# Attention's tail takes up the first slots of sequence 0 and turns six sequences' tokens, in a fused transformer block on one core

## The chip, the cores and the metric

The kernel runs on one core of a Trainium2 chip. The metric is the device time of one execution, in microseconds; the median of three runs before the change is 558.34 us (557.69 to 560.09).

## The reference, cut to what matters

Eight sequences of 256 tokens with 192 features, all in fp32, pass through three residual parts. First a token mixer with one attention head (the embedding is gathered, two layer norms over the whole sequence). Then an attention with 12 heads of 16 features, whose queries and keys are RMS-normed. Last a two-level soft mixture of experts. The change stands between the last two parts, so these are what must be seen:

```
h = h + attn(layernorm(h))          # 12 heads: softmax(q k) v, then a projection
xg = l2norm(layernorm(h)) * sqrt(192) * gamma_in   # groups of 64 tokens
phi = l2norm(slots1) * sqrt(192)                   # 128 slots
logits1 = xg @ phi.T
disp1 = softmax(logits1, over the 64 tokens)       # dispatch
comb1 = softmax(logits1, over the 128 slots)       # combine
slots = disp1.T @ xg;  yn = l2norm(slots) * sqrt(192) * gamma2
... second-level slots, 32 experts, and comb1 mixes their output back
```

## The kernel before, in words

The program is a sequence of blocks: `mixer_and_attention`, `first_slots`, `second_slots`, `second_dispatch`, `experts`. In a block each engine has its own instruction list, written out by hand, and waits on semaphores; an engine executes its list in order. A block ends when all engines have ended their lists, and the next begins together on all of them.

**Attention.** One sequence n is one call of `body(n)` on PE, ACT and DVE, and the bodies overlap by hand. Twelve heads are three quads of four heads, a quad q is two pairs u of two heads. `scores_and_maxima(score, best)` (L579 to L618) issues for one pair the plain products whose row maxima DVE wants (L604, into PSUM banks `MAXES` = 0, 1) and for an earlier pair the products with the maximum folded in (L611, into `SCORES` = 2, 3). DVE's `row_max` (L1141) reduces a pair's 128x1024 products. When a quad's two pairs have their maxima, PE's `turn_max` (L626) transposes them through bank 2 and DVE's `keep_max` (L1146) writes them into the queries. ACT's `expo` (L916; L920 in two halves for the second pair) takes the exponentials out of banks 2 and 3 into `prob`. PE's `mix` (L643) multiplies them by the values into banks 4 and 5. The next quad's `expo` waits for the `mix` of the quad before, since `prob` has one buffer for each pair; the next pair's scores wait for the `expo` of the pair before, since there is one pair of score banks. After a sequence's third `mix` come `keep_out` (ACT, L925), `turn_out` (PE, L653), `divide` (DVE, L1153 and L1157), `turn_mixed` (PE, L662), `keep_mixed` (ACT, L930), `project` (PE, L672), `add` (DVE, L1164), `out_stats` (DVE, L1172 and L1175), `root_out` (ACT, L936 and L939) and `make_tokens` (POOL, L330 and L334). In `body(n)` these steps of sequence n-1 are interleaved with the quads of n, as are the steps that make the queries, keys and values of n+1, which use banks 6 and 7 (`FRONT`).

In the last body, n = 7, there is no next sequence, and `keep_busy` (L97, matmuls of the identity whose results nobody reads) stands in those places; it stands too between all steps behind it (L758 to L769). After `project(7)` PE issues ten of them, and the block ends with `root_out(7)` on ACT. POOL has made tokens 0 to 6 by then.

**First slots.** For each n, PE turns the tokens (`turn`, L1350, into bank 3, `TURN`), ACT copies them (`keep`, L1459), PE makes the logits (`logits`, L1365, banks 1, 2 or 6, 7), DVE takes their maxima (`maxima`, L1528 and L1530), ACT the exponentials for dispatch (L1468) and combine (L1476), PE turns the dispatch weights (`turn_disp`, L1384, bank 3), DVE copies them (L1546) and inverts the sums (L1535), POOL scales the combine weights (`scale_comb`, L1611), PE turns these (`turn_comb`, L1375, bank 3) and DVE copies them (L1539). PE makes the slots (`make_slots`, L1395), ACT squares them (L1486) and takes their factors (L1491, L1494), DVE norms them (`norm_slots`, L1552). PE averages and turns them. The list is a loop over n (L1427) in which iteration n holds `logits(n)`, `turn(n + 2)`, `make_slots(n - 1)`, `turn_comb(n - 1)`, `make_means(n - 2)` and `turn_disp(n)`. POOL makes the tokens of sequence 7 (`make_x`, L1600 and L1604) before the first `scale_comb`. SP issues three loads of 576 KB for the second slots when the block begins.

## Time and profile before

| what | value |
|---|---|
| median of 3 runs | 558.34 us (557.69 to 560.09) |
| the profiled execution | 555.03 us |
| its span in the trace | 553.3 us |
| mean granted TensorE clock | 0.997 |
| attention's last body to the end of its block | about 239.9 to 271.5 us |
| first slots | 271.5 to 326.0 us |
| second slots, second dispatch | 326.0 to 409.5 us |
| experts and the end | 409.5 to 553.3 us |

Times in the views are microseconds from the start of the span. PE is TensorE's matmul, PEld its weight load, DVE VectorE, ACT ScalarE, POOL GpSimd, SP SyncE. "PEclk" is the clock that TensorE was granted, 1.00 being full. A matmul of fp32 operands shows as two instructions, so the counts of PE are twice those in the code. Matmuls are pipelined: the duration of a group of them reaches a little into the next group, so where the order is plain the starts of two groups are the better measure. In brackets stands the engine's idle time ahead of an instruction and what ended it.

### The profile page before, as it was taken

To read this page: it belongs to the slowest core of one execution; us is meant where nothing else is said; L and a number is where in the kernel's file an instruction comes from. 1 tells how busy PE (TensorE), PEld (TensorE's weight loads), DVE (VectorE), ACT (ScalarE), POOL (GpSimd) and SP (SyncE) were. 2 spreads that over 40 slices of the span, in tenths; PEclk is the share of its full clock that TensorE was granted. 3 is DMA by queue.
4 is the path that set the end of the run, shared out by engine and by line. 5 is a ranking of instruction groups with operands and counts; after the bars stand their busy time and mean duration, and the time that the engine had idled before them with its cause. 6 is when DMAs were issued, how large, how long until landed. Compare 5 with 4: busy or idle time off the path is not lost. (4 is left out here: it accounts for less than half of the span.)

```text
span 553.3 us, 13531 instructions
## 1 busy us (share of the span) xinstructions
PE 518.4 (94%) x5431; PEld 424.2 (77%) x5431; DVE 313.4 (57%) x738; ACT 256.3 (46%) x822; POOL 83.4 (15%) x136
## 2 busy tenths in 40 slices
PE   6999999999999999999888779899989999999997
PEld 5888888866566566666765545788879999999986
DVE  3348679676877776663246745566734444443443
ACT  1234344366656656644267647576642323232320
POOL 6480000011044034321201100011000000000000
PEclk9999999999999999999989999999999999999999
DMA  6180000000000000000300225011239999999733
GB/s 243 51 285 2 2 0 2 1 1 1 1 2 2 2 1 1 1 2 1 109 22 10 77 77 168 2 59 58 83 150 408 364 355 347 330 319 314 223 53 121
DMA packets 20721, 58.79 MB, mean 106 GB/s; under 512 B 3042, under 2 KB 9796, under 8 KB 20548
## 3 DMA queue, kind: packets, MB, share of 16 engines
q1 hardware_dynamic: 14756, 49.47, 24.9%
q0 software_dynamic: 1056, 4.33, 4.1%
q10 hardware_dynamic: 4848, 4.13, 2.6%
q8 instruction: 43, 0.70, 0.6%
q14 instruction: 18, 0.15, 0.1%
HBM read 53.21 MB, written 4.33 MB: 104 GB/s over the span
## 5 line engine op out<-in xcount | busy, mean ns | idle before, releaser
L2096 PE MATMUL banks<-slots_t,w 64*128 64x128 f32 x1536 | 91.4, 272 | 1.1 <-PEq L1807 1.1
L2096 PEld LDWEIGHTS banks<-slots_t,w 64*128 64x128 f32 x1536 | 90.1, 188 | 1.5 <-issue 1.3
L1141 DVE TENSOR_REDUCE qk<-banks 128x4 f32<-128x1024 f32 x48 | 58.9, 1226 | 39.5 <-PE banks L604 39.5
L2169 ACT ACTIVATE ex_gelu<-banks,b_sb 128x128 f32<-128x128 f32 x128 | 36.5, 368 | 90.1 <-PE banks L2096 90.1
L604 PE MATMUL banks<-qk_t 16*128 16x256 f32 x384 | 54.4, 400 | 2.6 <-DVE qk L1141 2.4
L611 PE MATMUL banks<-qk_t 17*128 17x256 f32 x384 | 54.4, 400 | 0.0
L2189 DVE SCALAR_TENSOR_TENSOR ex_act_t<-banks,b_sb,ex_gelu 128x128 f32<-128x128 f32 x128 | 36.1, 345 | 28.7 <-ACT ex_gelu L2169 28.7
L604 PEld LDWEIGHTS banks<-qk_t 16*128 16x128 f32 x384 | 33.2, 184 | 20.3 <-issue 13.7
L2127 PE MATMUL banks<-w,ex_act_t 64*128 64x192 f32 x512 | 47.1, 323 | 1.0 <-DVE ex_act_t L2189 1.0
L2199 DVE TENSOR_REDUCE ex_rows<-banks 128x192 f32<-128x384 f32 x32 | 17.9, 558 | 47.5 <-PE banks L2127 47.5
L2127 PEld LDWEIGHTS banks<-w,ex_act_t 64*128 64x128 f32 x512 | 41.0, 187 | 1.2 <-issue 1.2
L920 ACT ACTIVATE wk_t<-banks 128x512 f32<-128x512 f32 x48 | 26.1, 595 | 32.8 <-PE banks L611 32.8
L916 ACT ACTIVATE wq_t<-banks 128x1024 f32<-128x1024 f32 x24 | 24.6, 1024 | 26.0 <-PE banks L611 25.6
L344 POOL TENSOR_TENSOR qk<-qk,att_rms 128x384 f32<-128x384 f32 x14 | 11.4, 838 | 150.5 <-ACT att_rms L892 150.5
L611 PEld LDWEIGHTS banks<-qk_t 17*128 17x128 f32 x384 | 32.8, 184 | 1.0 <-DVE qk_t L1146 0.4
L97 PE MATMUL banks<-ident 128*128 128x128 f32 x208 | 27.5, 279 | 0.0
L97 PEld LDWEIGHTS banks<-ident 128*128 128x128 f32 x208 | 24.9, 192 | 2.6 <-issue 2.6
L643 PE MATMUL banks<-wq_t,val 128*32 128x256 f32 x192 | 25.4, 385 | 0.1
L643 PE MATMUL banks<-wk_t,val 128*32 128x256 f32 x192 | 25.4, 385 | 0.0
L2218 POOL DMA_DIRECT2D yn_all<-rows_scratch x7 | 3.5, 499 | 120.4 <-DMA rows_scratch<-ex_rows 120.4
L539 PE MATMUL banks<-qkv_w_sb,w_t 128*128 128x384 f32 (+1 forms) x64 | 19.1, 420 | 0.0
L330 POOL TENSOR_SCALAR centred<-h,out_mv,out_factor 128x192 f32<-128x192 f32 x14 | 14.0, 1007 | 21.6 <-ACT out_factor L939 21.6
(237 smaller groups left out, 1026.5 us busy)
## 6 DMA issues: line engine op xcount, KB each, us to landing
w<-in_w SPq DMA_DIRECT2D x32, 768.0 KB, 10.0
w<-in_w2e SPq DMA_DIRECT2D x32, 384.0 KB, 10.8
w_slot<-in_w_slot SPq DMA_DIRECT2D x8, 576.0 KB, 3.9
rows_scratch<-ex_rows ACTq DMA_DIRECT2D x28, 96.0 KB, 7.1
yn_all<-rows_scratch POOLq DMA_DIRECT2D x7, 384.0 KB, 9.7
out<-h SPq DMA_DIRECT2D x8, 192.0 KB, 1.9
qkv_w_sb<-in_qkv_w SPq DMA_DIRECT2D x1, 864.0 KB, 4.9
wk_t<-in_wk_t ACTq DMA_DIRECT2D x2, 289.5 KB, 3.5
```

Source lines behind the costliest of these rows:

```text
L97: nc.tensor.matmul(g.ps[bank][:, 0:P], g.ident[:, :], g.ident[:, :], start=True, stop=True)
L539: last = nc.tensor.matmul(g.ps[banks[t]][:, 0:cols.stop - cols.start], x_t[:, 2 * t, :], g.t["qkv_w"][:, 2 * t, cols], start=True, stop=False)
L604: last_best = nc.tensor.matmul(g.ps[MAXES[hh]][:, half * SEQ:(half + 1) * SEQ], g.qk_t[bn_ % 2][row:row + HDIM, bq, 0, half * P:(half + 1) ...
L611: last_score = nc.tensor.matmul(g.ps[SCORES[hh]][:, half * SEQ:(half + 1) * SEQ], g.qk_t[n % 2][row:row + HDIM + 1, q, 1, half * P:(half + ...
L643: last = nc.tensor.matmul(bank[32 * j:32 * j + 32, (q % 2) * SEQ:(q % 2 + 1) * SEQ], val[n % 2][:, m, QH * q + j, :], prob[j // 2][:, j % ...
L916: nc.scalar.activation(prob[u][:, :, :, :].rearrange("p a b n -> p (a b n)"), flat(SCORES[0], SCORES[1] + 1), ACT.Exp).then_inc(S["exped"], 1)
L920: nc.scalar.activation(prob[u][:, hh, :, :].rearrange("p b n -> p (b n)"), g.ps[SCORES[hh]][:, :], ACT.Exp).then_inc(S[done], 1)
L1141: nc.vector.tensor_reduce(to, flat(MAXES[0], MAXES[1] + 1).rearrange("p (h t n) -> p h t n", h=2, n=SEQ), AX.X, ALU.max, negate=True).then ...
L2096: return nc.tensor.matmul(bank[:, j * P:(j + 1) * P], g.w1[n % BUFS][rows, first + j * P:first + (j + 1) * P], x, start=start, stop=stop, ...
L2127: last = nc.tensor.matmul(out_bank(n, half)[:, 0:DIM], act_t[n % 2][rows, j * P:(j + 1) * P], g.w2[e][rows, j, :], start=(j == 0), stop=(j ...
L2169: nc.scalar.activation(gelu[n % 2][:, j * P:(j + 1) * P], gate_bank(n)[:, j * P:(j + 1) * P], ACT.Gelu_apprx_tanh, bias=g.t["b1"][:, n, HB ...
L2189: nc.vector.scalar_tensor_tensor(out=act_t[n % 2][:, j * P:(j + 1) * P], in0=value_bank(n)[:, j * P:(j + 1) * P], scalar=g.t["b1"][:, n, j ...
```

## The change

- `first_slots`' helpers become functions of their own (`turn_tokens`, `keep_tokens`, `slot_logits`, `logit_maxima`, `disp_exponentials`, `comb_exponentials`, `turn_dispatch`, `keep_dispatch`, `invert_comb`), and their tiles and semaphores become shared ones. The turned tokens get a buffer for each sequence (`x_t`), in the memory of the first experts' weights, as do `comb`, `disp_t` and `disp`. `logit_banks(n)` is (0, 1) or (6, 7); `MEANS` is bank 2.
- Attention's last body (`last_body` on PE, ACT and DVE, `END` = 7) has two pairs of score banks: the second pair of each quad goes to `FRONT` (so does that of the last quad of sequence 6), where its `expo` is one instruction over 1024 columns. Scores wait for the exponentials of two pairs before instead of one. All `keep_busy` from there on are gone but four.
- In the tail PE also turns the tokens of sequences 0 to 5, DVE copies them (ACT did), and sequence 0 goes as far as its dispatch weights and its inverted combine sums; the logits of sequence 1 are the last thing that PE does in the block.
- `first_slots` loops from n = 1. Only tokens 6 and 7 are turned there, through bank 2. POOL scales the combine weights of sequence 0 before it makes the tokens of sequence 7.

The core of the diff (the functions moved out of `first_slots` keep their bodies and are left out):

```diff
@@ attention, PE
+        def two_pairs(n, q):
+            return n == END or (n == END - 1 and q == QUADS - 1)
+        def score_banks(n, q, u):
+            return FRONT if u and two_pairs(n, q) else SCORES
...
-                    if count:
+                    if n == END:
+                        pe.wait_ge(S["exped"], count - 1)
+                    elif count and score_banks(n, q, u) == SCORES:
                         pe.wait_ge(S["exped"], count)
...
             def turn_max(n, q):
-                if count:
+                if n == END:
+                    pe.wait_ge(S["exped"], 2 * count - 1)
+                elif count:
                     pe.wait_ge(S["half_exped"], count)
...
+            def last_body():
+                n = END
+                scores_and_maxima((n - 1, 2, 0), (n, 0, 1))
+                pe.wait_ge(S["fill_kept_s"], 2 * n + 2)
+                pe.wait_ge(S["fill_kept_v"], n + 1)
+                keep_busy(nc, g, FRONT[0], 4)
+                turn_max(n, 0)
+                scores_and_maxima((n - 1, 2, 1), (n, 1, 0))
+                scores_and_maxima((n, 0, 0), (n, 1, 1))
+                mix(n - 1, 2)
+                scores_and_maxima((n, 0, 1), (n, 2, 0))
+                turn_max(n, 1)
+                turn_out(n - 1)
+                scores_and_maxima((n, 1, 0), (n, 2, 1))
+                mix(n, 0)
+                scores_and_maxima((n, 1, 1), None)
+                pe.wait_ge(S["maxed"], 2 * QUADS * BATCH)
+                tokens_ahead(0, MAXES[0])
+                turn_mixed(n - 1)
+                turn_max(n, 2)
+                tokens_ahead(1, MAXES[1])
+                mix(n, 1)
+                scores_and_maxima((n, 2, 0), None)
+                project(n - 1)
+                scores_and_maxima((n, 2, 1), None)
+                pe.wait_ge(g.x_kept, 2)
+                slot_logits(nc, g, 0)
+                pe.wait_ge(S["exped"], 2 * QUADS * BATCH - 1)
+                tokens_ahead(2, MEANS)
+                mix(n, 2)
+                tokens_ahead(3, TURN)
+                turn_out(n)
+                pe.wait_ge(g.x_kept, 3)
+                tokens_ahead(4, MEANS)
+                turn_mixed(n)
+                pe.wait_ge(g.x_kept, 4)
+                pe.wait_ge(g.first["disp_exped"], GPS)
+                turn_dispatch(nc, g, 0)
+                project(n)
+                pe.wait_ge(g.x_kept, 5)
+                tokens_ahead(5, MEANS)
+                slot_logits(nc, g, 1)
@@ attention, ACT
+            def last_body():
+                n = END
+                expo(n - 1, 2, 0)
+                root_out(n - 2)
+                expo(n - 1, 2, 1)
+                expo(n, 0, 0)
+                keep_out(n - 1)
+                expo(n, 0, 1)
+                expo(n, 1, 0)
+                keep_mixed(n - 1)
+                expo(n, 1, 1)
+                expo(n, 2, 0)
+                root_out(n - 1)
+                expo(n, 2, 1)
+                keep_out(n)
+                disp_exponentials(nc, act, g, 0)
+                keep_mixed(n)
+                comb_exponentials(nc, g, 0)
+                root_out(n)
@@ attention, DVE
+            def last_body():
+                n = END
+                row_max(n, 0, 1)
+                keep_max(n, 0)
+                row_max(n, 1, 0)
+                row_max(n, 1, 1)
+                row_max(n, 2, 0)
+                keep_max(n, 1)
+                divide(n - 1)
+                row_max(n, 2, 1)
+                keep_tokens(dve, nc.vector.tensor_copy, g, 0, MAXES[0])
+                keep_max(n, 2)
+                keep_tokens(dve, nc.vector.tensor_copy, g, 1, MAXES[1])
+                add(n - 1)
+                out_stats(n - 1)
+                logit_maxima(nc, dve, g, 0)
+                keep_tokens(dve, nc.vector.tensor_copy, g, 2, MEANS)
+                keep_tokens(dve, nc.vector.tensor_copy, g, 3, TURN)
+                divide(n)
+                keep_tokens(dve, nc.vector.tensor_copy, g, 4, MEANS)
+                keep_dispatch(nc, dve, g, 0)
+                invert_comb(nc, dve, g, 0)
+                add(n)
+                out_stats(n)
+                keep_tokens(dve, nc.vector.tensor_copy, g, 5, MEANS)
@@ first_slots, PE
-            turn(0)
-            keep_busy(nc, g, 6, 3)
-            turn(1)
-            for n in range(BATCH + 3):
-                if n < BATCH:
+            for n in range(1, BATCH + 3):
+                if 2 <= n < BATCH:
                     logits(n)
-                if n + 2 < BATCH:
-                    turn(n + 2)
+                if n == 2:
+                    last_tokens(BATCH - 1)
...
+                if n == 1:
+                    last_tokens(BATCH - 2)
@@ first_slots, ACT
-            keep(0)
-            keep(1)
-            for n in range(BATCH + 2):
+            for n in range(1, BATCH + 2):
                 if n < BATCH:
-                    disp_exp(n)
-                if n + 2 < BATCH:
-                    keep(n + 2)
-                if 0 <= n - 1 < BATCH:
+                    disp_exponentials(nc, act, g, n)
+                if n == 2:
+                    keep_tokens(act, nc.scalar.copy, g, BATCH - 1, MEANS)
+                if n - 1 < BATCH:
                     squares(n - 1)
                     root_slots(n - 1)
+                if n == 1:
+                    keep_tokens(act, nc.scalar.copy, g, BATCH - 2, MEANS)
@@ first_slots, POOL
-            for n in range(MADE_AHEAD, BATCH):
-                make_x(n)
-            for n in range(BATCH):
+            scale_comb(0)
+            make_x(BATCH - 1)
+            for n in range(1, BATCH):
                 scale_comb(n)
```

## Rows read from the trace of the kernel before

**Rows 1.** The page: the engines' busy time, and the chain that ended last, by line.

```profile
PE 518.4 (94%) x5431; PEld 424.2 (77%) x5431; DVE 313.4 (57%) x738; ACT 256.3 (46%) x822; POOL 83.4 (15%) x136
...
PE banks L2096 16%; PE banks L2127 8%; PE banks L2135 1%; DMA yn_all<-ex_rows 1%; DVE ex_rows L2199 0%; DVE h L2209 0%; ACTq L2071 0%; ACT ex_gelu L2169 0%; DVE ex_act_t L2189 0%; DVEq L2188 0%
```

**Rows 2.** Busy time by stretch: stretch, length, busy us (count) of each engine, PEclk, DMA share, GB/s.

```profile
258.00:271.50 13.50, 13.00 (x108) 10.70 (x104) 2.87 (x11) 4.37 (x9) 3.00 (x3) 1.00 0.01 1
283.00:299.00 16.00, 12.90 (x121) 9.34 (x121) 10.19 (x33) 11.40 (x61) 1.84 (x3) 1.00 0.01 2
278.00:279.00 1.00, 1.00 (x8) 0.78 (x7) 0.00 (x0) 0.00 (x0) 0.61 (x1) 0.50 0.03 14
```

**Rows 3.** The timeline of PE, attention's last body and tail: start, us, line, tiles, count [idle before].

```profile
239.90 0.48 PE L604 MATMUL banks<-qk_t 16*128 16x256 f32 x2
...
244.82 0.41 PE L643 MATMUL banks<-wq_t,val 128*32 128x256 f32 x2
...
245.82 0.48 PE L604 MATMUL banks<-qk_t 16*128 16x256 f32 x2
...
248.37 0.48 PE L604 MATMUL banks<-qk_t 16*128 16x256 f32 x2 [0.15 <-DVE qk L1141]
...
257.69 1.13 PE L611 MATMUL banks<-qk_t 17*128 17x256 f32 x8
...
264.25 0.87 PE L653 MATMUL banks<-ident,wv_t 128*128 128x128 f32 x6
...
266.12 0.64 PE L662 MATMUL banks<-ident,w 128*96 128x128 f32 x4
...
267.43 1.57 PE L672 MATMUL banks<-proj_t_sb,xt 96*128 96x192 f32 x8
...
268.84 2.39 PE L97 MATMUL banks<-ident 128*128 128x128 f32 x20
```

**Rows 4.** The timeline of ACT in the same stretch.

```profile
245.95 0.80 ACT L925 COPY wv_t<-banks 128x768 f32<-128x768 f32 x1 [1.19 <-PE banks L643]
...
247.06 1.02 ACT L916 ACTIVATE wq_t<-banks 128x1024 f32<-128x1024 f32 x1 [0.30 <-PE banks L611]
...
266.80 0.58 ACT L930 COPY xt<-banks 96x512 f32<-96x512 f32 x1 [2.60 <-PE banks L662]
...
270.89 0.20 ACT L939 ACTIVATE out_factor<-att_out_log 128x2 f32<-128x2 f32 x1
```

**Rows 5.** The timeline of DVE: a row maximum, attention's last addition, a copy of 384 columns.

```profile
241.08 1.23 DVE L1141 TENSOR_REDUCE qk<-banks 128x4 f32<-128x1024 f32 x1 [0.31 <-PE banks L604]
...
269.04 0.56 DVE L1164 TENSOR_TENSOR h<-h,banks 128x384 f32<-128x384 f32 x1 [2.98 <-PE banks L672]
...
322.48 0.56 DVE L1641 COPY w<-banks 128x384 f32<-128x384 f32 x1
```

**Rows 6.** The timeline of PE and ACT where the first-slots block begins.

```profile
271.54 0.52 PE L1350 MATMUL banks<-ident,tokens 128*128 128x128 f32 x3 [0.30 <-PEq L103]
...
272.15 0.48 ACT L1459 COPY fs_x_t<-banks 128x384 f32<-128x384 f32 x1 [1.05 <-PE banks L1350]
...
275.60 0.93 ACT L1468 ACTIVATE fs_disp_t<-banks,fs_neg_slot 128x64 f32<-128x64 f32 x4 [1.86 <-DVE fs_neg_tok L1530]
...
277.04 0.41 PE L1384 MATMUL banks<-ident,fs_disp_t 128*128 128x128 f32 x2 [1.80 <-ACT fs_x_t L1459]
```

**Rows 7.** The timeline of DVE and POOL in that block's loop: maxima, and scaled combine weights.

```profile
306.62 0.41 DVE L1528 TENSOR_REDUCE fs_neg_slot<-banks 128x4 f32<-128x256 f32 x1
...
285.42 0.61 POOL L1611 TENSOR_TENSOR fs_comb<-fs_comb,fs_comb_inv 128x256 f32<-128x256 f32 x1 [6.74 <-DVE fs_comb_inv L1535]
...
306.79 0.61 POOL L1611 TENSOR_TENSOR fs_comb<-fs_comb,fs_comb_inv 128x256 f32<-128x256 f32 x1 [4.73 <-DVE fs_comb_inv L1535]
...
311.62 0.61 POOL L1611 TENSOR_TENSOR fs_comb<-fs_comb,fs_comb_inv 128x256 f32<-128x256 f32 x1 [4.22 <-DVE fs_comb_inv L1535]
...
316.46 0.61 POOL L1611 TENSOR_TENSOR fs_comb<-fs_comb,fs_comb_inv 128x256 f32<-128x256 f32 x1 [4.22 <-DVE fs_comb_inv L1535]
```

More of the change, by code:

```diff
@@ L97, in keep_busy, with logit_banks, turn_tokens, keep_tokens @@
         nc.tensor.matmul(g.ps[bank][:, 0:P], g.ident[:, :], g.ident[:, :], start=True, stop=True)
+def logit_banks(n):
+    return (0, 1) if n % 2 == 0 else (6, 7)
+def turn_tokens(nc, g, n, bank):
+    for c in range(3):
+        last = nc.tensor.transpose(g.ps[bank][:, c * P:(c + 1) * P], g.tokens[n][:, 1 + c * P:1 + (c + 1) * P],
+                                   g.ident[:, :])
+    last.then_inc(g.x_turned, 1)
+def keep_tokens(eng, copy, g, n, bank):
+    eng.wait_ge(g.x_turned, n + 1)
+    copy(g.x_t[n][:, :, :], g.ps[bank][:, 0:3 * P].rearrange("p (c n) -> p c n", c=3)).then_inc(g.x_kept, 1)
@@ new lines, in slot_logits @@
+def slot_logits(nc, g, n):
+    for part in range(2):
+        for to_slots in (True, False):
+            for t in range(TPS):
+                rows, c = ((slice(0, P), 2 * t), (slice(0, REST) if t == 0 else slice(REST, P), 1))[part]
+                of_x, of_phi = g.x_t[n][rows, c, :], g.phi_t[rows, c, :]
+                lhs, rhs = (of_phi, of_x) if to_slots else (of_x, of_phi)
+                first = 0 if to_slots else P
+                last = nc.tensor.matmul(g.ps[logit_banks(n)[t]][:, first:first + P], lhs, rhs,
+                                        start=(part == 0 and to_slots), stop=(part == 1),
+                                        skip_group_check=True)
+    last.then_inc(g.first["logits"], 1)
@@ new lines, in logit_maxima, with disp_exponentials @@
+def logit_maxima(nc, dve, g, n):
+    dve.wait_ge(g.first["logits"], n + 1)
+    both = g.psum[:, logit_banks(n)[0]:logit_banks(n)[1] + 1, :]
+    nc.vector.tensor_reduce(g.neg_slot[:, n, :, :], both[:, :, 0:P].rearrange("p t (h n) -> p t h n", h=2),
+                            AX.X, ALU.max, negate=True).then_inc(g.first["maxed"], 1)
+    nc.vector.tensor_reduce(g.neg_tok[:, n, :], both[:, :, P:2 * P],
+                            AX.X, ALU.max, negate=True).then_inc(g.first["maxed"], 1)
+def disp_exponentials(nc, act, g, n):
+    act.wait_ge(g.first["maxed"], 2 * n + 2)
+    if n >= 2:
+        act.wait_ge(g.first["disp_turned"], n - 1)
+    for gr in range(GPS):
+        t, half = gr // 2, gr % 2
+        nc.scalar.activation(g.disp_t[n % 2][:, gr * GROUP:(gr + 1) * GROUP],
+                             g.ps[logit_banks(n)[t]][:, half * GROUP:(half + 1) * GROUP], ACT.Exp,
+                             bias=g.neg_slot[:, n, t, half:half + 1]).then_inc(g.first["disp_exped"], 1)
@@ new lines, in comb_exponentials, with turn_dispatch @@
+def comb_exponentials(nc, g, n):
+    for t in range(TPS):
+        nc.scalar.activation(g.comb[n % NC][:, t, :], g.ps[logit_banks(n)[t]][:, P:2 * P], ACT.Exp,
+                             bias=g.neg_tok[:, n, t:t + 1], accum_out=g.comb_sum[:, n, t:t + 1]
+                             ).then_inc(g.first["comb_exped"], 1)
+def turn_dispatch(nc, g, n):
+    for t in range(TPS):
+        last = nc.tensor.transpose(g.ps[TURN][:, t * P:(t + 1) * P],
+                                   g.disp_t[n % 2][:, t * P:(t + 1) * P], g.ident[:, :])
+    last.then_inc(g.first["disp_turned"], 1)
@@ L675, in project, with warm @@
                 last.then_inc(S["projected"], 1)
-            def warm(n, first, last):
+            def warm(n, first):
                 if n == 0 and first:
@@ L755, in _ @@
             keep_busy(nc, g, OUT[0], 11)
-            for n in range(BATCH):
+            for n in range(END):
                 body(n)
-            scores_and_maxima((BATCH - 1, 2, 0), None)
-            keep_busy(nc, g, 0, 4)
-            scores_and_maxima((BATCH - 1, 2, 1), None)
-            keep_busy(nc, g, 0, 4)
-            mix(BATCH - 1, 2)
-            keep_busy(nc, g, 0, 4)
-            turn_out(BATCH - 1)
-            keep_busy(nc, g, 0, 4)
-            turn_mixed(BATCH - 1)
-            keep_busy(nc, g, 0, 3)
-            project(BATCH - 1)
-            keep_busy(nc, g, 0, 10)
+            last_body()
         @block.scalar
@@ L980, in _ @@
                 token_body(i, more=i + 1 < BATCH // WIDE)
-            for n in range(BATCH):
+            for n in range(END):
                 body(n)
-            expo(BATCH - 1, 2, 0)
-            root_out(BATCH - 2)
-            expo(BATCH - 1, 2, 1)
-            keep_out(BATCH - 1)
-            keep_mixed(BATCH - 1)
-            root_out(BATCH - 1)
+            last_body()
         @block.vector
@@ L1281, in _ @@
                 stats(i, 1)
-            for n in range(BATCH):
+            for n in range(END):
                 body(n)
@@ L1474, in comb_exp @@
                     act.wait_ge(S["comb_turned"], n - NC + 1)
[L1475 to L1478 removed]
+                comb_exponentials(nc, g, n)
             def squares(n):
```

249 lines of the change are left out of this document (91 added, 158 removed).

## The prediction, made before the changed kernel was seen

> **What bounds the kernel now.** I read first the chain that ended last and the busy times of the page. The last quarter of the span is PE at the experts' products [rows 1], and ahead of it the program is a row of blocks, each of which begins when all engines have ended the one before. So a microsecond saved before the experts is a microsecond of the whole, provided that the block it is in ends earlier. The page shows the sum (PE 94% of the span, [rows 1]), and the table of windows two kinds of stretch [rows 2]. In attention's tail (258 to 271.5) PE looks full, 13.00 of 13.50 us, but DVE has 2.87 us of work and ACT 4.37: much of PE's time there is `keep_busy`. In the loop of the first slots (283 to 299) no engine is full: 12.90 of 16 on PE, 10.19 on DVE, 11.40 on ACT. Both are chains of short steps that hand over from engine to engine, so I follow the chains in the timelines.
>
> **The old tail.** A round of scores starts at 239.90, those of quads 0 and 2 of sequence 7 at 245.82 and 257.69 [rows 3]: 11.87 us for two quads. Behind the last quad come `turn_out` at 264.25, `turn_mixed` at 266.12, `project` at 267.43, then 20 instructions of filler from 268.84 [rows 3], beside which `add` starts at 269.04 [rows 5] and `root_out` ends at 270.89 + 0.20 = 271.09 [rows 4]. The next block starts at 271.54 [rows 6], 0.45 us after that. I call this distance the handover.
>
> **The old start of the first slots.** Sequence 0 walks alone through turn (271.54), copy (272.15), logits, exponentials (275.60), turned weights (277.04) [rows 6]; the first combine scaling that has a full iteration behind it, that of sequence 1, comes at 285.42 [rows 7], 13.88 us after the block's start. PE idled 1.80 us ahead of 277.04 [rows 6], and just after it the granted clock is 0.50, the lower level of 1.2 GHz [rows 2]. From there the loop gives 285.42, 306.79 (four later), 311.62, 316.46 [rows 7]: 21.37 / 4 = 5.34 us an iteration as long as tokens are turned in it, 4.83 us in the last two, where they aren't. The difference of 0.51 is one copy of turned tokens on ACT, 0.48 [rows 6], which shares bank 3 with what comes next.
>
> **Part 1, the last body.** I schedule the new lists by hand. Constants: a round of scores keeps PE 1.10 (8 matmuls 1.13, [rows 3]); round start to exponential 1.24 (245.82 to 247.06), to row maximum 1.18 (239.90 to 241.08); exponential 1.02, row maximum 1.23, a wait across engines 0.05 to 0.15 (the round at 248.37 followed DVE by 0.14) [rows 3 to 5]; `mix` 1.00 (244.82 to 245.82), `mix` start to ACT 1.13 (245.95), `keep_out` 0.80 [rows 3, 4]; a `turn_max` about 0.35 and tokens 0.50 (three transposes are 0.52, [rows 6]). The half exponentials become one of 1024 columns, which the other pair's 1.02 already prices [rows 4]. Then:
> - Round A at 239.90; maximum until 242.31; `turn_max(7, 0)` to 242.80. Round B at 242.80, its maximum until 245.21. Round C waits for that, 245.35. `mix(6, 2)` 246.45 to 247.45. Round D waits for C's maximum, 247.90. `turn_max(7, 1)`, `turn_out(6)` (behind `keep_out(6)`, 248.60 to 249.40) to 250.30. Round E waits for D's maximum and `keep_max`, 250.85. In the old list the same maxima (the ones of pair 2, 1) were started at 251.74 by the pace of 5.93, so the maxima are only 0.9 ahead: with two pairs of score banks the single pair `MAXES` and DVE's 1.23 set the pace, 2.55 to 2.95 from round to round.
> - `mix(7, 0)` 251.95 to 252.95, `expo(7, 1, 0)` 253.08 to 254.10. Then ACT has `keep_mixed(6)` ahead of `expo(7, 1, 1)`, and PE turns tokens 0 before `turn_mixed(6)`: 254.05 + 0.50 + 0.68 (266.12 to 266.80, [rows 3, 4]) = 255.23 for the copy of 0.58, `expo(7, 1, 1)` 255.81 to 256.83, `mix(7, 1)` 256.90 to 257.90. Scores of quad 2 start at 257.90; before it was 257.69 [rows 3]. The two pairs of banks have gained nothing up to here.
> - `project(6)` now stands between the two rounds of quad 2 (259.00 to 260.41), and ACT has `root_out(6)` between the two exponentials. It waits for `add(6)`, 1.61 after the start of `project` (267.43 to 269.04), and ends 2.05 after the start of `add` (269.04 to 271.09) [rows 3 to 5]: 259.00 + 3.66 = 262.66. Then `expo(7, 2, 1)` to 263.68, `mix(7, 2)` 263.73, `keep_out(7)` from 264.86 to 265.66, `turn_out(7)` 265.72. From here the old distances hold: + 1.87 `turn_mixed` 267.59, + 1.31 `project` 268.90. It was 267.43: **attention ends 1.5 us later**.
> - The new work on that tail: logits 0 are eight matmuls of up to 0.24 (the filler's 2.39 / 10, [rows 3]), 1.65 to 1.9. With tokens 2 they lie on PE from 261.5 to 263.65 or 263.9, beside `root_out` and `expo`, for which PE waits until 263.73 anyway; without that cover all of 2.2 to 2.4 would show. Tokens 3 and 4 and the turned dispatch weights lie in PE's waits for ACT and DVE; five copies of 384 columns on DVE are 0.56 each [rows 5], all in DVE's idle time. The dispatch exponentials (0.93, [rows 6]) sit on ACT between `keep_out(7)`, over at 265.66, and `keep_mixed(7)`, due at 268.27: free. The combine exponentials sit before `root_out(7)`, which waits longer. Behind `project(7)` tokens 5 and logits 1 end at about 272.4, with `root_out(7)` at 268.90 + 3.66 = 272.56 and DVE's last copy beside it. Block start: 273.0, + 1.5.
>
> **Part 2, the first slots' start.** Tokens 0 and 1, logits 0 and 1 and all of sequence 0's dispatch are gone from it. At the start DVE takes the maxima of sequence 1 and PE makes slots 0. From maxima to the combine scaling of an iteration without tokens the trace has 306.62 to 311.62 [rows 7], 5.00 us. ACT has tokens 6 to copy (0.48) and the combine exponentials behind the factors, beside DVE's norming. POOL has 0.61 and the 3.00 of one sequence's tokens [rows 2, 7] before the scaling of sequence 1, over by 3.7. So the scaling of sequence 1 comes at 273.0 + 5.0 = 278.0, not at 285.42. Against the block's start that is 5.0 in place of 13.88, **- 8.9 us**. Bounds: 3.7, POOL's own work, if the chain were shorter than that, and 8.7, if POOL's work came ahead of the whole chain.
>
> **Part 3, the loop.** From sequence 1 to 7 the old loop needs 316.46 - 285.42 = 31.04 us [rows 7]. The new one has tokens only in iteration 2: 5.34 + 5 x 4.83 = 29.49, **- 1.5 us**. Bounds: 0, if the moved chain has no slack, and -2.1, if iteration 2 has it too.
>
> **The sum:** 1.5 - 8.9 - 1.5 = -8.9, taken as -9.0 with the schedule's roundings (307.5 for the last scaling, 316.46 before). The later blocks hold no wait on a fixed time: their loads are issued by the progress of slots and logits, so they move along. The profiled execution took 555.03 (span 553.3 and 1.7 around it), 3.3 below the median of 558.34; on its base the sum gives 546.0, on the median's 549.3. I forecast 549.3.
>
> **The clock.** The one half-speed second in this part of the trace came after an idle of 1.80 us on PE [rows 2, 6]. The new body has no filler: PE waits 1.45 us before round C, 0.45 before D, 0.55 before E, 0.9 before `mix(7, 1)`. The loop of the first slots, which has such waits in every iteration (12.90 of 16 us busy), kept the full clock [rows 2]. A stretch at half clock of the kind at 278 costs at most the PE work in it once more. The Trainium skill (TensorE: Matmul & The Clock Gate, "A second HAM failure mode: psum-queue depth-cycling") tells of a kernel whose small idles between groups of matmuls made the clock swing between its two levels. By that rule the change would pay in its last body; the loop of the first slots, with such idles and a full clock, so far speaks against it.
>
> **Rivals.** A fall of half a per cent, 2.8 us, is about what a measurement can tell from no change.
> - *The forecast, 63%*: 546 to 552. Part 2 is nearly sure, as the steps leave a chain in which nothing else ran.
> - *Clock swings in the new body, 15%*: the filler's removal costs one or two stretches at 1.2 GHz in rounds C to `mix(7, 1)`. The rounds, 1.10 each, and the mixes double for some 3.5 us each: + 1.7 to + 3.5, so 551 to 553. For it: the gap before round C. Against it: the loop.
> - *The tail is slower than my schedule, 10%*: PE's list holds `slot_logits(0)`, three turns of tokens and `turn_dispatch(0)` ahead of steps of the chain, and each waits on DVE copies. If each hit the chain, + 1.6 for the logits, + 2.0 for four turns, + 0.6 for `turn_dispatch`: 549.3 + 4.2 = 553.5.
> - *The gain is absorbed, 7%*: a later block waits for something that did not move (weight loads, the code of the new lists). Then 556 to 560, no change. Against it: no load is tied to absolute time, and the three loads at the block's start are needed 50 us later.
> - *Slower, 3%*: the clock stays at its lower level from round C through the whole loop. PE's work in an iteration, 12.90 / 16 of 4.83 = 3.9, becomes 7.8, so + 3.0 in each of six iterations, + 5 in the body: 549.3 + 18 + 5 = 572. It decides if the waits of the new lists keep PE from winning back the clock; before, it was back at 1.00 by 283 [rows 2].
> - *Faster than forecast, 2%*: 545.
>
> **How the numbers follow.** The likeliest is 549.3. The range goes from 545.5 (the profiled base, the exact sum) to 554.5, which takes in the clock and the slow tail. Faster by over 0.5%: the first three and the last, 0.90. Same: the absorbed case, 0.07. Slower: 0.03.
>
> **What would show it.** Right: first instruction of the new first slots 1 to 2 us later than 271.5; POOL's scaling of sequence 1 some 5.0 us behind it; iterations of 4.83 from sequence 3; scores of quad 2 of sequence 7 near 257.9; `expo(7, 2, 1)` ending with `root_out(6)` just ahead of it; granted clock 1.00 from 240 to 326. Wrong: a clock of 0.50 around 246 to 252 (clock rival); `turn_out(7)` waiting on PE's own list (tail rival); a distance from the first slots' start to the experts' start that shrank by less than 10 us while attention's did not grow (absorbed).

## The result, and the profile after

The changed kernel takes 553.85 us in the median of five executions (552.72 to 555.03); the kernel before took 557.69 beside it (556.17 to 560.09, five). The ratio is 0.9925, interval 0.9901 to 0.9948: faster by 0.75%, 3.8 us. The forecast was 549.3, a gain of 9.0. The profiled execution took 553.95 (span 552.1), against 555.03 (553.3) before. Its mean granted clock is 0.981 where it was 0.997, and all five executions lie between 0.978 and 0.981. An execution over 1.5% above the fastest of its kernel (two of the changed kernel's second set below, one with two fillers before D) counts in the medians here, but not in the ratios.

The trace of before is a quick one. The executions of that kernel that ran beside the experiments have a recorded clock too, 36 of them: 10 at 0.996 or 0.997 (555.1 to 556.5 us), 16 at 0.994 and 10 at 0.991 or 0.988 (up to 560.1). So between the two traces the gain is 1.1 us, between the medians 3.8.

**First slots: as forecast.** The timeline of POOL after the change; the last two lines answer to [rows 7]:

```profile
279.52 0.61 POOL L1695 TENSOR_TENSOR w<-w,comb_inv 128x256 f32<-128x256 f32 x1 [7.07 <-POOLq L190]
280.12 1.99 POOL L1684 TENSOR_SCALAR centred<-h,out_mv,out_factor 128x192 f32<-128x192 f32 x2
282.19 1.01 POOL L1688 TENSOR_TENSOR w<-centred,gamma_in_sb 128x384 f32<-128x384 f32 x1
284.61 0.61 POOL L1695 TENSOR_TENSOR w<-w,comb_inv 128x256 f32<-128x256 f32 x1 [1.40 <-DVE comb_inv L184]
289.82 0.61 POOL L1695 TENSOR_TENSOR w<-w,comb_inv 128x256 f32<-128x256 f32 x1 [4.60 <-DVE comb_inv L184]
294.65 0.61 POOL L1695 TENSOR_TENSOR w<-w,comb_inv 128x256 f32<-128x256 f32 x1 [4.22 <-DVE comb_inv L184]
...
313.98 0.61 POOL L1695 TENSOR_TENSOR w<-w,comb_inv 128x256 f32<-128x256 f32 x1 [4.22 <-DVE comb_inv L184]
```

The first line is sequence 0's scaling, at the block's start. That of sequence 1 follows 5.09 us later (forecast 5.0, before 13.88), and POOL waited 1.40 for it, so its work on tokens 7 is hidden. The six iterations to 313.98 take 29.37 (forecast 29.49, before 31.04): one of 5.21, five of 4.83.

**Attention's last body: not as forecast.** The timeline of PE; these lines answer to [rows 3] and the first of [rows 6]:

```profile
241.11 0.48 PE L703 MATMUL banks<-qk_t 16*128 16x256 f32 x2
...
246.49 0.80 PE L703 MATMUL banks<-qk_t 16*128 16x256 f32 x2 [1.41 <-DVE qk L1278]
...
258.19 2.08 PE L710 MATMUL banks<-qk_t 17*128 17x256 f32 x8
...
263.54 0.41 PE L744 MATMUL banks<-wq_t,val 128*32 128x256 f32 x2 [0.53 <-ACT wk_t L1043]
...
264.54 1.13 PE L710 MATMUL banks<-qk_t 17*128 17x256 f32 x8
...
275.56 1.57 PE L773 MATMUL banks<-proj_t_sb,xt 96*128 96x192 f32 x8 [0.45 <-ACT xt L1057]
...
279.54 0.93 PE L1513 MATMUL banks<-tokens,w 64*128 64x193 f32 x8 [0.54 <-PEq L190]
```

Round A starts at 241.11, not 239.90. The change touches nothing ahead of it, and in the twelve other traces below it starts at 240.00 to 241.60: these 1.2 us are the spread of executions, with before at its early end. Round C waits 1.41, as forecast (1.45). But its first pair of products takes 0.80, not 0.48, and the eight of a round 2.08 against 1.13 at 264.54. From A to the scores of quad 2 are 23.43 us, forecast 18.0, before 17.79; from A to the block's end 38.43, before 31.64. The windows of the same trace, their columns those of [rows 2], give the cause:

```profile
245.00:246.00 1.00, 0.09 (x4) 0.00 (x0) 0.88 (x1) 0.82 (x1) 0.92 (x2) 1.00 0.00 0
246.50:247.00 0.50, 0.50 (x4) 0.50 (x8) 0.00 (x0) 0.00 (x0) 0.47 (x1) 0.50 0.00 0
247.00:262.00 15.00, 15.00 (x105) 8.92 (x100) 5.43 (x7) 3.78 (x5) 0.00 (x0) 0.50 0.00 1
262.00:263.00 1.00, 1.00 (x5) 0.61 (x3) 0.42 (x1) 1.00 (x2) 0.00 (x0) 0.50 0.00 0
263.00:263.50 0.50, 0.01 (x1) 0.00 (x0) 0.45 (x1) 0.49 (x1) 0.00 (x0) 0.58 0.00 0
264.00:300.00 36.00, 30.39 (x270) 22.45 (x264) 21.12 (x65) 20.39 (x93) 8.95 (x11) 1.00 0.14 51
```

The granted clock falls to 0.50, the level of 1.2 GHz, just ahead of round C, and stays there for 17 us, in which PE, once round C has begun, is busy without a gap (15.00 of 15.00) until 263.0. It is back at 2.4 GHz only at 263.4, in the wait ahead of `mix(7, 1)`. DVE and ACT, the pace in the forecast, are busy for 5.43 and 3.78 of those 15 us: PE has become the bound. A second, short stretch at half clock lies at 314.6 to 318, behind the last scaling; twelve of its transposes (`turn_yn`) take 2.30 where they took 1.53:

```profile
314.00:316.00 2.00, 2.00 (x18) 1.09 (x18) 0.96 (x4) 0.91 (x6) 0.59 (x1) 0.65 0.00 0
316.00:318.00 2.00, 2.00 (x16) 1.60 (x9) 1.18 (x5) 1.08 (x8) 0.00 (x0) 0.50 0.67 197
```

**The account.** + 1.2 ahead of round A, + 6.8 in the last body, - 10.48 from the block's start to the last scaling (34.44 after, 44.92 before), + 0.2 in the rest of the first slots: the second slots start at 323.74 instead of 326.04, - 2.3. The experts' last products stand at 534.93 instead of 537.17, so that survives; the final DMA of `yn_all` takes 0.9 longer (5.84 against 4.92), and the span is 1.2 shorter.

### The profile page after: what moved, and what is told of

Same layout as the page of the kernel before. It is cut to its first block and busy times, and to the rows that moved or that the text cites. A ratio compares the mean times of both kernels' runs of the same rounds, so it can differ in the third digit from the quotient of the medians.

```text
span 552.1 us, 13341 instructions
## 1 busy us (share of the span) xinstructions
PE 516.6 (94%) x5343; PEld 419.2 (76%) x5343; DVE 317.0 (57%) x744; ACT 253.6 (46%) x812; POOL 84.2 (15%) x136
## 5 line engine op out<-in xcount | busy, mean ns | idle before, releaser
L703 PE MATMUL banks<-qk_t 16*128 16x256 f32 x384 | 57.2, 416 | 3.7 <-DVE qk L1278 3.7
L710 PE MATMUL banks<-qk_t 17*128 17x256 f32 x384 | 58.1, 422 | 0.0
L703 PEld LDWEIGHTS banks<-qk_t 16*128 16x128 f32 x384 | 34.6, 192 | 22.4 <-issue 15.7
L710 PEld LDWEIGHTS banks<-qk_t 17*128 17x128 f32 x384 | 34.8, 195 | 1.7 <-issue 1.4
L1047 ACT ACTIVATE wk_t<-banks 128x512 f32<-128x512 f32 x40 | 21.7, 595 | 27.9 <-PE banks L710 27.9
L744 PE MATMUL banks<-wq_t,val 128*32 128x256 f32 x192 | 27.1, 406 | 0.5 <-ACT wk_t L1043 0.5
L744 PE MATMUL banks<-wk_t,val 128*32 128x256 f32 x192 | 27.1, 406 | 0.0
L744 PEld LDWEIGHTS banks<-wq_t,val 128*32 128x32 f32 x192 | 9.4, 113 | 11.2 <-ACT wk_t L1047 4.1
L2114 POOL TENSOR_TENSOR comb_t<-comb_t,sd_inv_row 128x256 f32<-128x256 f32 x8 | 4.9, 612 | 81.7 <-DVE sd_inv_row L2073 81.7
```

The costliest lines, as they stand in the source:

```text
L703: last_best = nc.tensor.matmul(g.ps[MAXES[hh]][:, half * SEQ:(half + 1) * SEQ], g.qk_t[bn_ % 2][row:row + HDIM, bq, 0, half * P:(half + 1) ...
L710: last_score = nc.tensor.matmul(g.ps[score_banks(n, q, u)[hh]][:, half * SEQ:(half + 1) * SEQ], g.qk_t[n % 2][row:row + HDIM + 1, q, 1, ha ...
L744: last = nc.tensor.matmul(bank[32 * j:32 * j + 32, (q % 2) * SEQ:(q % 2 + 1) * SEQ], val[n % 2][:, m, QH * q + j, :], prob[j // 2][:, j % ...
L1047: nc.scalar.activation(prob[u][:, hh, :, :].rearrange("p b n -> p (b n)"), g.ps[SCORES[hh]][:, :], ACT.Exp).then_inc(S[done], 1)
```

## The experiments

Where not said otherwise an experiment is the changed kernel with its edit. Times are medians, each set beside the kernel before on the same chip: 557.15 for the first four runs, 557.3 for the next four, 557.25 for the three after, 556.79 for the last. "Clock" is the mean granted clock of an execution. A round is called by its letter in the prediction, A to E. My theory: the clock costs the missing 5 us, since the body lost its filler. The rivals: the two pairs of score banks or the steps put into the tail delay the chain; or PE's many small products lose the clock whether it idles or not.

**Filler before round C alone.**

```diff
                 scores_and_maxima((n - 1, 2, 1), (n, 1, 0))
+                keep_busy(nc, g, SCORES[1], 5)
                 scores_and_maxima((n, 0, 0), (n, 1, 1))
```

> Five matmuls of filler (about 1.2 us) stand in PE's idle time before round C, where the granted clock fell to 0.50 in the changed kernel (246.3 to 263.3). Theory 'clock': this one idle stretch costs the 17 us at the lower level; with filler the clock stays at 1.00 through the last body, attention's end comes some 5.3 us earlier and the time is about 548.5 (ratio to the kernel before near 0.984). Rival 'order': the new lists themselves are slow (bank pairs, the steps put ahead of the chain), the clock is only a symptom of idle waits; the filler stands in idle time and changes nothing: 553 to 555.

Measured: 549.66 (546.24 to 552.62), ratio 0.9852 (0.9795 to 0.9909); clocks 1.0, 0.994, 0.991, 0.985, with the times in the same order: 546.24, 548.05, 551.28, 552.62. The windows of the profiled execution (0.991):

```profile
245.00:258.00 13.00, 11.05 (x130) 7.40 (x130) 7.45 (x10) 6.19 (x7) 1.96 (x2) 1.00 0.00 1
258.00:260.00 2.00, 2.00 (x24) 1.16 (x15) 0.00 (x0) 0.23 (x1) 0.00 (x0) 1.00 0.00 0
260.00:263.00 3.00, 3.00 (x12) 2.47 (x12) 0.66 (x2) 0.79 (x1) 0.00 (x0) 0.50 0.00 0
263.00:266.00 3.00, 3.00 (x14) 2.24 (x12) 0.76 (x4) 1.48 (x3) 1.54 (x2) 0.50 0.00 0
266.00:270.00 4.00, 4.00 (x29) 2.03 (x27) 1.31 (x3) 0.00 (x0) 1.46 (x2) 0.50 0.02 4
```

The body held the clock for 14 us longer, then lost it at about 260, some 2.4 us behind the gap of 1.05 that precedes `mix(7, 1)` at 257.59, for 10 us. `project(7)` follows round A by 33.06 us, 34.45 in the changed kernel. The clock is the right suspect, but the gap before C isn't the only place.

**Filler in all four gaps.** Beside C: two before round D, two before E, three before `mix(7, 1)`.

```diff
+                keep_busy(nc, g, SCORES[1], 5)
                 scores_and_maxima((n, 0, 0), (n, 1, 1))
                 mix(n - 1, 2)
+                keep_busy(nc, g, FRONT[0], 2)
                 scores_and_maxima((n, 0, 1), (n, 2, 0))
...
                 turn_out(n - 1)
+                keep_busy(nc, g, SCORES[1], 2)
                 scores_and_maxima((n, 1, 0), (n, 2, 1))
...
                 tokens_ahead(1, MAXES[1])
+                keep_busy(nc, g, SCORES[1], 3)
                 mix(n, 1)
```

> Filler in all four gaps of the last body: 5, 2, 2 and 3 matmuls before rounds C, D, E and before the second mix. 'Clock': as with the first gap alone if that one decides (548.5); if the gaps work together, only this run keeps the clock and is about 5 us under the changed kernel while the run with the first gap alone isn't. Rival 'order': 553 to 555, or slower if the filler pushes the rounds.

Measured: 549.15 (548.86 to 550.24), ratio 0.9861 (0.9837 to 0.9886); clocks 1.0 once and 0.994 three times. The windows:

```profile
245.00:262.00 17.00, 16.38 (x171) 11.53 (x171) 8.13 (x13) 6.84 (x8) 1.28 (x2) 1.00 0.00 1
262.00:273.00 11.00, 8.99 (x80) 6.95 (x79) 5.81 (x17) 4.82 (x15) 3.03 (x3) 1.00 0.01 2
305.00:314.00 9.00, 6.40 (x46) 4.61 (x48) 6.52 (x20) 4.74 (x24) 0.61 (x1) 0.81 0.24 80
```

and the timeline of PE, in which round A stands at 240.50:

```profile
258.10 1.13 PE L710 MATMUL banks<-qk_t 17*128 17x256 f32 x8
...
269.11 1.57 PE L773 MATMUL banks<-proj_t_sb,xt 96*128 96x192 f32 x8 [0.45 <-ACT xt L1061]
```

Body and tail keep 1.00; two stretches of 3 us at 0.50 lie behind them, at 308.4 to 311.4 in the first slots and at 397.4 to 400.5 ahead of the experts. Quad 2 follows A by 17.60 (forecast 18.0) and `project(7)` by 28.61 (forecast 29.0, changed kernel 34.45). The hand schedule was right, within 0.4 us, for the clock that it assumed.

**The kernel before without its last body's filler** (the filler behind that body stays).

```diff
             def warm(n, first, last):
...
-                if n == BATCH - 1 and last:
-                    keep_busy(nc, g, FRONT[0], last)
```

> The kernel before, without the filler inside its last body (the filler behind that body stays). 'Clock': the old body loses the clock as well, from about 243 on, and the whole gets 2 to 5 us slower than the kernel before: 560 to 563. Rival 'order' (or: only the two pairs of banks bring the idle that counts): the old body's gaps are small enough or don't matter, 557 to 558.5.

Measured: 562.89 (561.84 to 567.6), ratio 1.013 (1.0079 to 1.0181), 5.7 us slower; clocks 0.973 to 0.985. Its windows:

```profile
245.00:248.00 3.00, 2.17 (x26) 0.70 (x18) 1.65 (x2) 1.09 (x2) 2.39 (x3) 0.83 0.00 0
248.00:257.00 9.00, 9.00 (x68) 5.23 (x64) 3.74 (x5) 3.38 (x5) 0.00 (x0) 0.50 0.01 2
257.00:260.00 3.00, 3.00 (x28) 2.38 (x30) 1.23 (x1) 1.02 (x1) 0.00 (x0) 0.97 0.00 0
```

The same fall, at 247.0 for 10 us, in a kernel with no other part of the change. So neither the banks nor the tail's new steps are needed for it; the missing filler is enough. From round A (241.60) to the block's end it takes 35.17 us, 3.5 more than with its filler (31.64). The rest of the 5.7 lies elsewhere: this execution has two more low stretches, at 322 to 325.8 and 410 to 415.

**As with four fillers, and `root_out(6)` behind `expo(7, 2, 1)` on ACT.**

```diff
                 expo(n, 2, 0)
-                root_out(n - 1)
                 expo(n, 2, 1)
+                root_out(n - 1)
                 keep_out(n)
```

> As with all four fillers, and ACT's root_out of sequence 6 moved behind the last exponential. My schedule has that exponential waiting about 1.1 us (262.66 against 261.65) for project, add and statistics of sequence 6. If that step holds, this is 0.8 to 1.1 us under the run with all fillers; if the chain there runs over PE's logits and tokens instead, the difference is 0 to 0.3.

Measured: 548.6 (547.92 to 551.64), ratio 0.9857 (0.9817 to 0.9897). In the trace no change: A at 240.69, `project(7)` at 269.30, again 28.61 behind it. In both traces the last mix starts 23.44 behind A, straight behind PE's own logits and tokens 2, when its exponential has already ended: PE's list holds it, not `root_out`.

**The old last body with its filler, one pair of score banks, and the new tail.**

```diff
         def two_pairs(n, q):
-            return n == END or (n == END - 1 and q == QUADS - 1)
+            return False
...
+                keep_busy(nc, g, FRONT[0], 3)
                 turn_max(n, 0)
...
```

In its tail the last mix also stands ahead of tokens 2.

> The old last body (one pair of score banks, its filler, its order on PE, ACT and DVE) with the new tail behind it: tokens 0 and 1 in place of the last four fillers, the logits of sequence 0 behind the last scores, the rest as in the changed kernel. If the two pairs of score banks bring nothing, as my schedule has it (maxima and DVE set the pace), this is as fast as the changed kernel with all fillers, within 1 us: 548 to 550, ratio near 0.985. If they are worth something, it is 1 to 3 us slower, 550 to 552. Either way the clock stays at 1.00 in the body.

Measured: 548.35 (546.23 to 550.08), ratio 0.9838 (0.9811 to 0.9864); clocks 0.991 to 1.0. PE, with A at 240.40:

```profile
258.40 1.13 PE L708 MATMUL banks<-qk_t 17*128 17x256 f32 x8
...
268.62 1.57 PE L769 MATMUL banks<-proj_t_sb,xt 96*128 96x192 f32 x8 [0.45 <-ACT xt L1055]
...
272.60 0.93 PE L1511 MATMUL banks<-tokens,w 64*128 64x193 f32 x8 [0.54 <-PEq L190]
```

Quad 2 after 18.00 (two pairs of banks 17.60), `project(7)` after 28.22 (28.61): at full clock the two pairs gain 0.4 us up to quad 2, of which nothing is left at the end. The body and the tail keep 1.00 here too; the mean of 0.991 in the profiled execution comes from 306.1 to 312.0 and 398.3 to 401.5, behind them.

**As the one with `root_out(6)` moved, and `logits(0)` split around the last mix**, tokens 2 to 4 behind them; on DVE `divide(7)` comes ahead of the copy of tokens 3.

```diff
-                slot_logits(nc, g, 0)
-                pe.wait_ge(S["exped"], 2 * QUADS * BATCH - 1)
-                tokens_ahead(2, MEANS)
+                slot_logits(nc, g, 0, (0,))
                 mix(n, 2)
-                tokens_ahead(3, TURN)
+                slot_logits(nc, g, 0, (1,))
+                tokens_ahead(2, MEANS)
                 turn_out(n)
+                tokens_ahead(3, TURN)
```

> The run with fillers and root_out moved, and the logits of sequence 0 split: four matmuls before the last mix, four behind it with tokens 2; tokens 3 and 4 behind turn_out. My reading of the two runs with all fillers is that the last mix waited for PE's own logits and tokens as much as for root_out, so that moving one alone gave nothing. If so, the last mix, and attention's end, come about 1.1 us earlier than there: 547.5, ratio 0.983. If the last mix is held by something else (the last exponential later than I think), within 0.3 us of it.

Measured: 547.88 (547.43 to 551.5), ratio 0.985 (0.9821 to 0.9878). A at 241.13, then:

```profile
268.73 1.57 PE L774 MATMUL banks<-proj_t_sb,xt 96*128 96x192 f32 x8 [0.41 <-ACT xt L1062]
```

27.60 after A, 1.0 earlier than with the logits in one piece. The last mix starts 22.42 behind A, also 1.0 earlier: it was PE's own work ahead of it that lay on the path. In the medians the microsecond is lost in their spread.

**Filler before D, E and `mix(7, 1)`, none before C**, run twice.

```diff
                 mix(n - 1, 2)
+                keep_busy(nc, g, FRONT[0], 2)
...
                 turn_out(n - 1)
+                keep_busy(nc, g, SCORES[1], 2)
...
                 tokens_ahead(1, MAXES[1])
+                keep_busy(nc, g, SCORES[1], 3)
```

> Filler at rounds D and E and before the second mix (2, 2, 3 matmuls), none at round C. If the gap before round C alone makes the clock fall, it falls here as well, at the same place; and if filler of full 128x128 matmuls helps it back, the stretch at 0.50 is shorter than 17 us, in the region of 4 to 10: 550 to 553. If the later gaps count as much as the first, the clock doesn't fall: 549.

Measured: 546.96 (545.85 to 549.26, four), ratio 0.9826 (0.9793 to 0.9858); clocks 1.0 three times and 0.994. The windows:

```profile
244.00:246.00 2.00, 0.59 (x12) 0.27 (x8) 1.23 (x1) 1.02 (x1) 1.92 (x3) 1.00 0.00 0
246.00:262.00 16.00, 15.48 (x165) 10.77 (x162) 7.50 (x13) 6.26 (x7) 0.24 (x1) 1.00 0.00 1
262.00:273.00 11.00, 8.90 (x81) 6.89 (x80) 5.74 (x18) 4.83 (x15) 3.07 (x4) 1.00 0.01 2
```

and the timeline of PE, with round A at 240.38:

```profile
268.99 1.57 PE L773 MATMUL banks<-proj_t_sb,xt 96*128 96x192 f32 x8 [0.45 <-ACT xt L1060]
...
272.97 0.93 PE L1516 MATMUL banks<-tokens,w 64*128 64x193 f32 x8 [0.54 <-PEq L190]
```

PE idles before round C just as in the changed kernel (1.41 us; 0.59 busy of 2 us), and the clock stays at 1.00. The block ends 32.59 after A, against 38.43 in the changed kernel and 31.64 before: 5.8 of the 6.8 us are the clock's, 0.95 the schedule's. So that gap by itself need not bring it down.

> The kernel with filler at round D, round E and the second mix (2, 2, 3 matmuls) once more. Four executions had mean clocks of 1.00, 1.00, 1.00 and 0.994 and a median of 546.96. If these gaps are the ones whose filling keeps the clock, six more have clocks of 0.99 to 1.00 and a median of 546.5 to 548; if the four were luck, some fall to 0.984 or lower, as two of six did with filler at D alone, and take 552 or more.

Measured: 551.21 (546.86 to 553.51, six), ratio 0.9908 (0.9876 to 0.994); clocks 1.0 once and 0.991 five times. The profiled execution was the one at 1.0 and shows the first run's distances from A to 0.02 us. The median of 546.5 to 548 was missed, and the clocks came as expected: the first result was in part a draw of undisturbed executions, and over all ten the median is 549.6. Where the five at 0.991 lost the clock no trace shows. That mean fits a low of 10 us in the body (filler at C, 551.28 us) as well as two short ones behind it (old body, 549.42).

**Eight fillers before D alone.**

```diff
                 mix(n - 1, 2)
+                keep_busy(nc, g, FRONT[0], 8)
```

> Eight matmuls of filler at round D alone, behind the place where the clock has fallen. In the changed kernel PE was busy without a break for 15 us at 0.50 with small products (16 or 17 rows, or 32 columns). If what PE runs decides when the clock comes back, these eight (some 3.8 us at half speed) bring it back near 252 and the time is 551 to 553 although the filler delays round D by over 3 us. If the return has nothing to do with it, the delay is simply added: 556 to 558.

Measured: 551.75 (547.63 to 552.55), ratio 0.9913 (0.9886 to 0.994); clocks 0.988 to 0.997. In the profiled execution the body kept 1.00, its lows lie at 310 to 314 and 399 to 402, and `project(7)` stands 1.35 us further behind A than with the small fillers (29.96 against 28.61): a filler longer than its gap is on the path. Since the clock had not fallen ahead of the eight, the run leaves open whether such products bring it back.

**The changed kernel once more.**

> The changed kernel once more, unchanged, for a second trace and more executions. If the fall of the clock is bound to the gap before round C, the trace shows 0.50 from about 246 again, and every execution has a mean clock near 0.98 and a time of 552 to 555. If only chance put it there, the place moves or some executions keep 1.00 and take about 547.

Measured: 552.86 (547.3 to 557.77, six), ratio 0.9886 (0.9839 to 0.9933). Its windows:

```profile
246.00:248.00 2.00, 1.62 (x28) 1.15 (x32) 0.68 (x2) 0.09 (x1) 0.86 (x1) 1.00 0.00 0
248.00:261.50 13.50, 13.49 (x88) 8.31 (x80) 5.41 (x8) 4.73 (x6) 0.00 (x0) 0.50 0.01 1
261.50:264.00 2.50, 1.97 (x25) 1.10 (x24) 0.56 (x1) 0.53 (x1) 0.00 (x0) 0.97 0.00 0
```

The same program, and round C now runs at full clock; the fall comes at 248.0, and 13.5 us follow. Its executions by clock:

| clock | 1.0 | 0.985 | 0.984 | 0.984 | 0.972 | 0.972 |
|---|---|---|---|---|---|---|
| us | 547.3 | 553.62 | 551.35 | 552.11 | 557.0 | 557.77 |

A line through these six and the five of the first result has a slope of 3.6 us for each 0.01 of mean clock, and meets 1.0 at 546.9 (3.3 and 547.3 without the two at 0.972). The 36 executions of the kernel before give 3.5 us. One execution in eleven kept the clock, and it took 547.3. That is 2.0 below my forecast of 549.3, but 1.3 above the 546.0 that the same sum gives on the quick profiled execution, and 8.15 below the median of the nine executions of the kernel before at 0.997 (555.45).

**With split logits and six more fillers in the first slots' iteration n = 8.**

```diff
+                if n == BATCH:
+                    pe.wait_ge(F["comb_exped"], TPS * (BATCH - 1))
+                    keep_busy(nc, g, 0, 3)
                 if 0 <= n - 3 < BATCH:
                     turn_means(n - 3)
+                if n == BATCH:
+                    keep_busy(nc, g, 0, 3)
```

> The kernel with the split logits, with three matmuls of filler at each of two further idle places of PE, in the last iterations of the first slots, where the clock fell to 0.50 for 3 to 5 us in the traces of the changed kernel, of the one with all fillers and of the one with the old body. If these falls cost what the traces suggest (1 to 2 us each in the executions that have one), the median comes from 547.9 to about 547.0 and the mean clock is 1.00 in nearly all executions. If not, 547.9 as without.

Measured: 550.31 (548.5 to 552.28), ratio 0.9877 (0.9849 to 0.9905); clocks 0.996 to 1.0. The clock is held better than without them (0.988 to 1.0), yet the median is 2.4 us higher, where 0.9 lower was expected. Up to the experts nothing differs (last scaling 307.15 and 307.18). In the experts PE has gaps that the other lacks; the windows of this kernel, then that of the kernel without the six:

```profile
460.00:480.00 20.00, 19.03 (x301) 18.73 (x298) 7.89 (x25) 5.26 (x19) 0.49 (x1) 1.00 1.06 317
480.00:500.00 20.00, 19.41 (x313) 19.22 (x311) 8.39 (x25) 5.72 (x20) 0.49 (x1) 1.00 1.00 302
```

```profile
460.00:480.00 20.00, 20.00 (x319) 19.85 (x317) 8.20 (x25) 5.36 (x20) 0.48 (x1) 1.00 1.08 311
480.00:500.00 20.00, 20.00 (x322) 19.92 (x320) 8.42 (x25) 5.56 (x21) 0.48 (x1) 1.00 0.98 311
```

From its first product to the start of its last reduction into `ex_rows` on DVE, the experts' stage took 129.3 us before and after the change, 130.6 with the split logits and 132.0 with the six fillers more. It took 131.9 in the trace with `root_out(6)` moved, and 129.8 and 129.4 in the two traces of the one program with filler at D, E and `mix(7, 1)`. The DMA engines are full there (1.00 or so of their share). Why it varies is open; the six fillers are not shown to be the cause.

**Two fillers before D alone.**

```diff
                 mix(n - 1, 2)
+                keep_busy(nc, g, FRONT[0], 2)
```

> Two matmuls of filler (0.5 us) at round D alone, the smallest edit. If the clock in the last body depends on several gaps near each other, and round D's is the one that decides with C's, most executions keep the clock or have it down for a short time: 547 to 550. If each gap counts by itself, C's is still there and the time is 552 to 554 as in the changed kernel.

Measured: 551.16 (546.62 to 560.84), ratio 0.9854 (0.9812 to 0.9896); clocks 1.0, 1.0, 0.997, 0.985, 0.984, 0.963. In the profiled one (0.984) the clock falls at 247.4 and is low until 261.0, and again at 285 to 288.3. Here too the place moved, and three of the six executions escaped.

## Why the prediction was right or wrong

- **Part 2 and Part 3, right.** 5.09 against 5.0 and 29.37 against 29.49; the nearest rows, maxima to scaling and the iterations without tokens, were the right prices.
- **Part 1's schedule, right at full clock.** With filler, `project(7)` follows round A by 28.61, forecast 29.0. That two pairs of banks gain nothing was forecast, and the old body shows it to 0.4 us. One wait in it had the wrong owner: I put the last mix down to `root_out` and `expo`, with PE's logits just fitting beside them, and it is the logits and tokens 2 that hold it. Moving `root_out` alone gave nothing, splitting the logits 1.0 us.
- **The failed step is "The clock".** It priced the removed filler at nothing, on the ground that the loop of the first slots has such waits and kept 1.00. What the runs showed in its place: the body loses the clock for 17 us, and that costs 5.8 us. The waits were as forecast (1.41 against 1.45); the ground didn't bear. It was one execution: in traces of other kernels the first slots lost the clock too (285 to 288, 308 to 311, 306 to 312 above), and of 36 executions of the kernel before 26 have a mean clock of 0.994 or less, where the trace that I read has 0.997. The loop also runs other products, mostly of 64 and 128 rows, where the body has 16 and 17 rows in the rounds and 32 columns in the mixes (80 of the 88 instructions from 246.4 to 258); whether that matters was not tested. No row of the trace of before could price the removal, as its body was never without filler; baring it cost 5.7 us in the median, 3.5 of them in the trace's last body and tail.
- **The clock rival was the right mechanism at too low a price.** It had 15%, and took stretches of some 3.5 us, at + 1.7 to + 3.5, from the dip of [rows 2]. That 553.85 lies inside the forecast's outer range, and 0.85 above this rival's, is no merit of the forecast's own sum. The windows of the kernel before around it:

```profile
277.50:278.00 0.50, 0.50 (x6) 0.50 (x5) 0.48 (x2) 0.10 (x2) 0.00 (x0) 0.85 0.14 55
278.00:281.00 3.00, 3.00 (x17) 2.22 (x17) 0.76 (x2) 0.32 (x2) 0.61 (x1) 0.50 0.01 5
281.50:282.00 0.50, 0.33 (x5) 0.03 (x2) 0.00 (x0) 0.50 (x3) 0.00 (x0) 1.00 0.00 0
```

  There PE, busy without a gap, had the full clock back within 4 us. In the changed body it was as busy and stayed low for 17, at 5.8 us. The rule of the Trainium skill that stood beside this step (TensorE: Matmul & The Clock Gate, "A second HAM failure mode: psum-queue depth-cycling"), that small idles between groups of matmuls make the clock swing between its levels, is borne out in part. With idles of 1.41 us and less in the body the clock fell, in the changed kernel and in the bare old body. With filler in all of them it stayed at 1.00 in the body of all four such kernels traced. But where it fell, it fell once in the body and stayed low for 10 to 17 us; it did not swing.
- **The slow-tail rival** fell: from quad 2's scores to `project(7)` the changed kernel takes 11.02 us (264.54 to 275.56, with the clock back), forecast 11.00.
- The sum as measured: + 0.95 for the body's schedule - 10.48 for the first slots + 5.8 for the clock in the body + 0.2 for the rest of the slots + 1.2 ahead of the body = - 2.3 at the second slots.

Shown: the last body's missing filler costs the missing gain; the banks and the tail don't. Ten of the eleven executions of the changed kernel took 551.35 us or more, seven of the eight with filler in all four gaps (with or without `root_out` moved) 550.24 or less. Not shown: which of the gaps decides. Filler at C alone left a fall at 260, at D alone one at 247.4, and with D, E and `mix(7, 1)` but not C none was traced, in two executions at 1.0, while five of six executions of the repeat had a mean of 0.991. By its ratio of 0.9908 that repeat can't be told from the changed kernel (0.9925 and 0.9886).

**The best version.** With the split logits the kernel takes 547.88 (0.985 of before, 0.9821 to 0.9878), with the old body 548.35 (0.9838, 0.9811 to 0.9864); the intervals don't part them. Either is about 1.5% under the kernel before. Their intervals lie clear of the changed kernel's first (0.9901 to 0.9948), but not of its second (0.9839 to 0.9933). Each was run once, with six executions, and the repeat above shows how far such a median can move.

## What to carry to other kernels

Work that only keeps an engine busy is part of the schedule: before removing it, price the products that it protects at half clock, for the whole stretch and not for one short dip. One execution that kept the clock in a stretch with idle gaps is no evidence that gaps elsewhere are harmless: look at the mean clock of many. And where a kernel's executions differ in mean clock, sort them by it before comparing medians of four to six.

## What the runs showed of the hardware

- Once fallen to 1.2 GHz, PE stayed there 17 and 13.5 us (changed kernel, two executions), 13.5 (two fillers at D), 10 (filler at C) and 10 us (bare old body), with hardly a gap in its work. A busy share of 1.00 stood beside 0.50 there (15.00 of 15.00 us) as it does beside 1.00 in the experts (20.00 of 20.00).
- One program falls at 246.3 in one execution and at 248.0 in another, and has a mean clock of 1.0 in a third; its time runs from 547.3 to 557.77. A mean of 0.981 stands for 0.019 x 552 x 2 = 21 us at half clock, the 17 and the 3.4 of the two stretches above.
- The experts' stage varied by 2.7 us (129.3 to 132.0) with the clock at 1.00 and the DMA engines full, with no cause found. That is as much as many of the differences between medians here.
